# Seven 16-head attention stages: VectorE's small work per tile in another order, with the aggregation one slot later

## The reference, cut to what matters

```
q, k, v = x @ Wq (+bq), src @ Wk (+bk), src @ Wv        # src is x or the context
p = softmax(q @ k.T / sqrt(8))                          # 16 heads, 64 keys, some with a mask
o = (p @ v)                                             # denominators come out of the same matmul
x = layernorm(x + o @ Wo (+bo))                         # mean and variance over 128 features
```

## Time and profile before

| what | value |
|---|---|
| median of 3 runs | 4357.68 us (4356.09 to 4358.32) |
| span of the profiled execution | 4443.1 us, granted PE clock 0.914 over all of it |
| busy over the span | PE 3746.7, PEld 2747.7, DVE 3214.4, ACT 2236.5, POOL 1618.2 us |
| L0a, 21 to 340 us | PE busy 300.9 of 319 us, DVE 284.3, ACT 184.3, POOL 186.8 |
| L0x, 374 to 708 us | PE busy 302.2 of 334 us, DVE 274.8 |
| L1x, 1806 to 2106 us | PE busy 291.0 of 300 us, DVE 248.3 |
| L1f, 2123 to 2383 us | PE busy 256.5 of 260 us, DVE 228.2 |
| L2a, 2723 to 3038 us | PE busy 300.5 of 315 us, DVE 274.1 |
| L2x, 3057 to 3320 us | PE busy 256.6 of 263 us, DVE 229.3 |
| L3x, 3943 to 4303 us | PE busy 334.8 of 360 us, DVE 321.6, POOL 191.7 |

### The profile page before, as it was taken

One profiled execution on the slowest core, in us unless ns is written; L12 is line 12 of the kernel. 1 busy time (PEld: TensorE's weight loads), 2 busy tenths in 40 slices (PEclk: granted clock), 3 DMA queues, 4 the chain that ended last, 5 costly groups with the idle time before them and its releaser, 6 DMA issues. The chain is left out here.

```text
span 4443.1 us, 137315 instructions
## 1 busy us (share of the span) xinstructions
PE 3746.7 (84%) x48696; PEld 2747.7 (62%) x48696; DVE 3214.4 (72%) x7860; ACT 2236.5 (50%) x4080; POOL 1618.2 (36%) x2677
## 2 busy tenths in 40 slices
PE   8997997588369999899998775998999778879986
PEld 6775666355257877677676553776774344457764
DVE  7996886224468888688786267887886677769975
ACT  4554553234334444566784344656873355535553
POOL 4663343633611111122354442332222244435544
PEclk9998997799789999999997887999999888889998
DMA  2011112466410000111001760000102100000001
GB/s 75 26 34 47 38 36 60 131 195 173 117 32 1 0 0 0 37 42 37 17 17 35 215 177 16 14 14 24 33 26 66 37 0 0 0 18 23 22 16 38
DMA packets 293801, 209.56 MB, mean 47 GB/s; under 512 B 51136, under 2 KB 272192, under 8 KB 293440
## 3 DMA queue, kind: packets, MB, share of 16 engines
q1 hardware_dynamic: 233760, 157.72, 12.4%
q0 software_dynamic: 12288, 25.19, 1.9%
q10 hardware_dynamic: 47520, 23.60, 1.8%
HBM read 122.49 MB, written 54.53 MB: 40 GB/s over the span
## 5 line engine op out<-in xcount | busy, mean ns | idle before, releaser
L1354 DVE TENSOR_TENSOR L0f_G<-L0f_SG,L0f_psH 128x512 f32<-128x512 f32 x106 | 73.0, 689 | 230.2 <-ACT L0f_SG L1098 138.4
L2223 POOL TENSOR_TENSOR L1a_rs<-L1a_ag,eps 128x1 f32<-128x1 f32 x64 | 12.1, 190 | 475.8 <-DVE L1a_ag L2383 475.8
L937 POOL DMA_INDIRECT L0f_sorted_x<-X,L0f_IDX x128 | 123.3, 963 | 86.7 <-issue 34.1
L958 POOL DMA_INDIRECT L0f_YG<-L0f_sorted_y,L0f_IDY x128 | 124.5, 973 | 80.4 <-DMA L0f_sorted_y<-L0f_YB 43.2
L2310 PE MATMUL L1a_psO<-L1a_WO,L1a_OT 128*64 128x128 f32 x2048 | 125.9, 276 | 6.3 <-ACT L1a_OT L2334 5.0
L2244 PE MATMUL L1a_psF<-L1a_XT,L1a_WQ 128*128 128x256 f32 x512 | 130.6, 389 | 0.5 <-DVE L1a_KT L2199 0.5
L1032 PEld LDWEIGHTS L0f_psO<-L0f_WB,L0f_G 128*128 128x128 f32 x848 | 107.4, 197 | 37.0 <-issue 37.0
L2310 PEld LDWEIGHTS L1a_psO<-L1a_WO,L1a_OT 128*64 128x64 f32 x2048 | 110.6, 137 | 24.3 <-ACT L1a_OT L2334 22.8
L1914 PE MATMUL L3a_psH<-L3a_UT,L3a_WG 128*128 128x512 f32 x128 | 81.4, 722 | 50.1 <-DVE L3a_G L2027 48.6
L586 ACT ACTIVATE L3x_PT<-L3x_psP 128x512 f32<-128x512 f32 x128 | 69.5, 595 | 100.9 <-PE L3x_psP L521 100.9
L1032 PE MATMUL L0f_psO<-L0f_WB,L0f_G 128*128 128x128 f32 x848 | 108.6, 280 | 8.0 <-issue 8.0
(11 more groups left out here) (684 smaller groups left out, 12981.2 us busy)
## 6 DMA issues: line engine op xcount, KB each, us to landing
L0f_WB<-in_w12a SPq DMA_DIRECT2D x53, 312.0 KB
L0f_XB<-L0f_sorted_x SPq DMA_DIRECT2D x53, 256.0 KB
L0f_sorted_y<-L0f_YB ACTq DMA_DIRECT2D x53, 256.0 KB
L1m_WB<-in_w12b SPq DMA_DIRECT2D x37, 321.0 KB
L1m_XB<-L1m_sorted_x SPq DMA_DIRECT2D x37, 256.0 KB
L1m_sorted_y<-L1m_YB ACTq DMA_DIRECT2D x37, 256.0 KB
L0f_sorted_x<-L0f_AC SPq DMA_DIRECT2D x27, 256.0 KB
L1m_sorted_x<-L1m_AC SPq DMA_DIRECT2D x27, 256.0 KB
```

The lines of the kernel that those rows point to most:

```text
L937: nc.gpsimd.indirect_dma_start(out=sorted_x[p][:, :], out_offset=bass.IndirectOffsetOnAxis(ap=IDX[:, k, t:t + 1], axis=0), in_=X[:, t, :], ...
L958: nc.gpsimd.indirect_dma_start(out=YG[:, b % 4, k, t % TB, :], out_offset=None, in_=sorted_y[p][:, :], in_offset=bass.IndirectOffsetOnAxis ...
L1354: nc.vector.tensor_tensor(G[0:f, J % 2, c, :], SG[0:f, c, :], up, ALU.mult).then_inc(S["g_ready"].sem, 1)
```

## The change

In `small` the order becomes: reciprocal of T-2, aggregation of T-5 (whose statistics were taken in the slot before), normalised output of T-2, residual sum of T-4, [second norm's sum in L3x], statistics of T-4. The output of a pair and POOL's work for it move one slot later, since the aggregation does; that puts the output into slots of the other parity (from even to odd in L0a, L0x, L1x and L2a, from odd to even in L1f, L2x and L3x). The mean squares of L0a move two slots later, and L0a unrolls four more slots of tiles and loops 11 turns instead of 12. The drain of each stage is one slot longer, in L0a two.

```diff
-def long_pipeline(eng, slot, drain):
+def long_pipeline(eng, slot, drain, first=8):
-    first, turns = 8, 12
+    turns = (56 - first) // 4
...
-            drain = 5 + e + late + (1 if affine is not None else 0) + (2 if tally else 0)
+            drain = 6 + e + late + (1 if affine is not None else 0) + (3 if tally else 0)
...
-                        F = T - 5 - e - late
+                        F = T - 6 - e - late
...
-                        Z, Y = T + 4, T - 7
+                        Z, Y = T + 4, T - 9
...
                     def small(T):
-                        A, J = T - 2 - late, T - 4 - e - late
+                        A, J, H = T - 2 - late, T - 4 - e - late, T - 5 - e - late
...
                             nc.vector.reciprocal(rden[:, A.par], o3[:, :, 2 * HD:VW]).then_inc(S["recip"].sem, 1)
+                        if H.ok:
+                            made(dv, "bn", H.t + 1)
+                            pace(nc.vector, S)
+                            nc.vector.bn_aggr(mv[:, H.u, H.par, :], st6[:, H.par, :]).then_inc(S["stats"].sem, 1)
+                        if A.ok:
+                            made(dv, "recip", A.t + 1)
+                            made(dv, "o_ready" if ln_o else "o_turned", A.t - 1)
+                            nc.vector.tensor_tensor(ON[:, A.par, :].rearrange("p (b h d) -> p b h d", h=2, d=HD),
+                                                    o3[:, :, 0:2 * HD].rearrange("p b (h d) -> p b h d", h=2),
+                                                    rden[:, A.par].unsqueeze(3).to_broadcast([P, HP, 2, HD]), ALU.mult).then_inc(S["normed"].sem, 1)
...
                             nc.vector.tensor_tensor(RB[:, J.u, J.par, :], psJ, res, ALU.add).then_inc(S["res"].sem, 1)
-                        if A.ok:
-                            made(dv, "recip", A.t + 1)
...
-                        if J.ok:
-                            made(dv, "res", J.t + 1)
-                            nc.vector.bn_stats(st6[:, J.par, :], RB[:, J.u, J.par, :]).then_inc(S["bn"].sem, 1)
...
                         if J.ok:
-                            made(dv, "bn", J.t + 1)
-                            pace(nc.vector, S)
-                            nc.vector.bn_aggr(mv[:, J.u, J.par, :], st6[:, J.par, :]).then_inc(S["stats"].sem, 1)
+                            made(dv, "res", J.t + 1)
+                            made(dv, "stats", J.t - 1)
+                            nc.vector.bn_stats(st6[:, J.par, :], RB[:, J.u, J.par, :]).then_inc(S["bn"].sem, 1)
...
-                        A = T - 5 - e - late
+                        A = T - 6 - e - late
```

More of the change, by code:

```diff
@@ L322, in slot @@
                             sp.dma_start(CR[:, N.u, :], io["ctxT"][:, bass.ds(N.p * 256, 256)]).then_inc(parity_sem("ctx_in", N), 16)
-                    long_pipeline(sp, slot, drain)
+                    long_pipeline(sp, slot, drain, 12 if tally else 8)
                     if arrive:
@@ L425, in slot @@
                             mean_squares(Y.p, X[:, bass.ds(Y.p * 2, 2), :], 1, MS[:, Y.u, :], "stat2_root", "means2")
-                    long_pipeline(g, slot, drain)
+                    long_pipeline(g, slot, drain, 12 if tally else 8)
                 @block.tensor
@@ L555, in slot @@
                             nc.tensor.matmul(psJ, OT[:, A.par, :], o, start=True, stop=True).then_inc(S["proj"].sem, 1)
-                    long_pipeline(pe, slot, drain)
+                    long_pipeline(pe, slot, drain, 12 if tally else 8)
                 @block.scalar
@@ L607, in slot @@
                             rows_of_x(M)
-                    long_pipeline(act, slot, drain)
+                    long_pipeline(act, slot, drain, 12 if tally else 8)
                 @block.vector
@@ L710, in slot @@
                             m.then_inc(S["out_rows"].sem, 1)
-                        for V_, par, mean, st, tallied, rooted in ((T + 3, 1, MC, stat2, "means", "stat_root"), (T - 8, 0, MS, stat, "means2", "stat2_root")):
+                        for V_, par, mean, st, tallied, rooted in ((T + 3, 1, MC, stat2, "means", "stat_root"), (T - 10, 0, MS, stat, "means2", "stat2_root")):
                             if tally and T.par == par and V_.ok:
@@ L720, in slot @@
                             nc.vector.tensor_scalar(MF[:, M.u, :], MI[:, M.u, :], 0.0, None, ALU.not_equal).then_inc(S["mask_used"].sem, 1)
-                    long_pipeline(dv, slot, drain)
+                    long_pipeline(dv, slot, drain, 12 if tally else 8)
             S.advance(dict.fromkeys(("xs", "rstd", "var_eps", "out_rows", "f_tx", "f_k", "f_q", "f_v", "o_tx", "o_k", "o_q", "o_v"), PAIRS))
```

## The result

| | median, us | lowest to highest | runs |
|---|---|---|---|
| before | 4357.72 | 4356.09 to 4358.32 | 4 |
| after | 4308.65 | 4300.37 to 4309.4 | 4 |

The ratio is 0.9879, interval 0.9867 to 0.9891: 49 us faster, forecast 33. A second measurement of the same kernel beside experiments gave 4303.91 (4297.26 to 4311.76; before there 4356.83), ratio 0.9874 (0.9856 to 0.9892).

A forecast was written before the change was run, and what follows sets the result against it. PE and DVE pass a token in L2a, L0a and L3x (9.91 us per pair in L2a, PE alone 9.47). Terms 17 + 10 + 3 = 30 us, 34 with half the loop edge back; 33 taken, 4325 us, range 4305 to 4347.

The forecast's parts named there:

- The token loop: L2a, L0a, L3x: PE and DVE wait for each other once per pair; 9.91 us in L2a, 8.84 after.
- the odd loop of 9.56: L0a: loop from odd scores including the reciprocal of mean squares, 0.1 us over PE's own time, left to rounding.
- rivals 1 and 2: 1: PE's chain through ACT holds the pair, 4350 to 4358, chance 0.09. 2: output waits for POOL, about 4385, 0.04.
- Rival 3: Loop body: new dependent DVE neighbours cost 0.44 us instead of 0.32, smaller gain, 4335; chance 0.20.
- Rival 4: All waits vanish and the loop edge costs nothing in L0a and L2a: 43 us, 4314; chance 0.12.
- I take the whole 7.2, since L3x shows it in the same code.: L0a and L2a: loop edges cost up to 0.3 us per turn, subtracted from 24.3 us, leaving 17.
- In these four nothing that DVE does sooner can be passed on, or very little.: L0x, L1x, L1f, L2x: 1 to 5 us from the odd slot near a loop edge, 3 taken.
- two waits of PE: L3x: 0.45 us for rope before V's projection and 0.12 from projection to scores, about 10 us gained.
- the output alone takes 0.52 us out of that slot: L3x, behind the odd residual sum: output, aggregation and normalised output leave the slot, covering both of PE's waits.
- DVE's total: DVE's work per slot: 0.24 us removed, at most 0.24 added, gain 0 to 0.1, only slack.
- The drain rule: Skill's flush after every VectorE instruction: loop saving would be 0.43 us instead of 0.55, DVE's work would not shrink.
- 4410 for the span of the next profile: Profiled span of 4443.1 us, 2% above the runs' median, less the forecast 33 us.

The follow-up runs named there:

- order_only: Kernel before with the residual sum put behind the normalised output, aggregation still right behind the statistics, no shift by a slot; 4371.36 us, ratio 1.0032.
- extra_work3: Changed kernel with VectorE writing zeros to an unread 128x384 scratch behind each tile's statistics, 448 times; 4367.63 us, ratio 1.0028.
- turn8: Changed kernel with loops turning every eight slots instead of four, and a semaphore instruction ahead of POOL's large operations; 4303.51 us, ratio 0.9874.
- output_later: Kernel before with output, drain and tally one slot later as in the change, order inside a slot unchanged; 4340.75 us, ratio 0.9967.
- sum_first: Changed kernel with the residual sum back ahead of the normalised output, aggregation still between reciprocal and residual sum; 4320.0 us, ratio 0.9907.

## Why the prediction was right in direction and too small

**The token loop was read rightly.** Both engines waited for each other once per pair, the loop through the residual sum was 9.91 us, and PE's own 9.47 came next. Measured after: 9.46 in L2a, and 9.51 in L0a, where in the odd slots the scores still start 0.15 us after the end of the shift and 0.37 to 0.39 after the projection (medians of the loop): the odd loop of 9.56 that the forecast let pass as rounding. DVE's piece measured 0.55 for 0.52. Of the rivals 1 and 2 nothing shows: the list of waits has none of PE between 2640 and 2880 us in L2a and between 60 and 300 us in L0a, and an output waited for POOL once per stage (in L1f twice), by 0.5 to 2.7 us, and nowhere inside the stretches of L0a, L2a and L3x read here. Rival 3's cost exists (in the loops of L1x, L1f, L2a and L2x of order_only the reciprocal and the output that needs it are 0.37 us or more apart), but an aggregation stands there in the changed kernel, and extra_work3 shows that L2a would not have noticed. Rival 4, no edge cost in L0a and L2a, is what happened in those two stages; it had been given 0.12 and 4314 us, and the median came out lower still.

**The step that failed: "I take the whole 7.2, since L3x shows it in the same code."** L0a and L2a gave 26.7 us. The gross sum of the forecast was 24.3, and the subtraction was wrong: turn8 shows no edge cost in these two stages. L3x and L0x have it for a reason of their own. There PE's last wait before the branch, for ACT's copy, is released late, and what the sequencer still has to do before the next scores comes after it; in L0x before, 1.07 us pass from that release (500.58) to the scores (501.65):

```profile
500.69 0.41 PE L434 MATMUL L0x_psF<-W,L0x_XS 128*128 128x128 f32 x2 [0.46 <-ACT L0x_CT L600]
500.93 0.39 PE L555 MATMUL L0x_psP<-W,L0x_OT 128*128 128x128 f32 x2
501.65 0.69 PE L482 MATMUL L0x_psS<-KB,L0x_QT 32*64 32x256 f32 x16 [0.33 <-issue]
```

In L0a and L2a of the changed kernel the lists named above have no such wait. That turn8 shortened L0x by 3.2 us bears it out; that this is the reason was only read from the trace. The stages gave 48.6 us for the forecast's sum of 30 (33 was that with half of the edge given back). Of the 18.6 missed this term is 7.2, and 2.4 more are in the periods: the shifts of L2a and L0a now lie 9.41 and 9.45 us apart per pair over the whole stage, under the 9.47 that was taken as PE's floor from one pair.

**The second, and the larger: "In these four nothing that DVE does sooner can be passed on, or very little."** Forecast 3 us, measured 12.2 (8.0 by the second pair of profiles), of it 4.7 in L2x, 4.1 in L0x, 2.2 in L1f. I had taken "PE busy 120.00 of 120" in L1f for a bound and L2x for a case of the same; L2x was busy 118.41 of 120 (3120 to 3240 us), and is 120.00 now. What the four stages had can be read from start-to-start times. In the loops of L2x before, the scores came 0.32 to 0.34 us after the projection in three slots of four, and 0.55 to 0.73 us in the first slot of each turn; in the changed kernel it is 0.32 in all. Before, and now:

```profile
3187.95 0.39 PE L555 MATMUL L2x_psP<-W,L2x_OT 128*128 128x128 f32 x2
3188.52 0.69 PE L482 MATMUL L2x_psS<-KB,L2x_QT 32*64 32x256 f32 x16 [0.18 <-issue]
```

```profile
3068.47 0.39 PE L555 MATMUL L2x_psP<-W,L2x_OT 128*128 128x128 f32 x2
3068.78 0.69 PE L482 MATMUL L2x_psS<-KB,L2x_QT 32*64 32x256 f32 x16
```

Over the loops that is 3.4 of the 4.7 us: a cost at the loop's edge, but in a stage for which the forecast had none, and one that DVE's earlier work removed. output_later alone removed it too (0.32 us in that slot, L2x -2.9). Which of PE's waits was released late there isn't shown. In L0x, PE's wait for ACT's copy of x's rows ahead of L445, 2.4 us in 12 waits, is down to 0.5 in one; of the stage's 4.1 us 1.2 lie in the loops, 1.3 in the first slots and 1.6 in the last. L1f's 2.2 and L1x's 1.2 us are near what a stage varies by, though four slots of L1f went from 16.18 to 16.09 us with PE busy 120.00 of 120 in both.

**L3x was right in size (9.6 for 10), in part by luck.** The forecast had two waits of PE, 0.45 us for rope (8.1 us in 18 pairs) and 0.12 at the scores (2.2). Start to start over the 24 pairs of the loops, product to V's projection fell from 30.4 to 22.8 us, a gain of 7.6; the odd scores come 0.22 us after the projection instead of 0.45 (medians), a gain of 5.3; and product to L441 rose from 25.0 to 29.5, a loss of 4.5 that the forecast didn't have. So one term was right, one too small and one missing, and the last two in part cancel. The cause is also narrower than written: "the output alone takes 0.52 us out of that slot" was the largest part of it, but output_later has the output gone and wins 1.4 us in L3x, and sum_first has the aggregation gone from behind the statistics as well and stands at 354.6, 2.2 above before. The output lands in the slot of L441, and PE waits for rope there. The gain is there only when the normalised output is also ahead of the wait.

**DVE's total.** The price of the neighbours was right (0.31 to 0.33 and 0.44 us in order_only). What I had not seen is that DVE is close behind PE in L1f and L2x, by 0.24 us per slot as extra_work3 has it; an order that had added more than it removed would have lost there, as order_only did.

**The drain rule.** The trace kept against it: 0.20, 0.31 and 0.43 us behind the same statistics, by what follows. The Trainium skill, "VectorE: DVE Perf Modes", section "The DRAIN you can't avoid", has every VectorE instruction followed by a flush of the pipeline, tied by a semaphore or not; the same section adds that a next instruction that isn't held starts earlier, which the prediction left out. By the flush alone order_only would have cost nothing and the change's new order would have saved less. The runs don't agree with that: order_only lost 14 us.

**The span.** "4410 for the span of the next profile": it was 4298.6. The step was that the 85 us by which the profiled span lay above the median would come again. They were that execution's own: every later span lies 2 us or less below its run's time, and most of the excess was in the work between L0x and L1x.

**How the gain adds up.** By the sums of the seven stages: output_later -15.4 us; from there to sum_first, which moves the aggregation away from the statistics, another -21.0; from there to the changed kernel -12.1, of which 11.9 in L3x. That is the 48.6.

## What to carry to other kernels

- Where two engines wait for each other by turns, add up the loop through both and compare it with each engine's own period; what counts is the work between the wait of one and the signal to the other, and an edit that looks like reordering can take it out of there. Small work that needs nothing goes ahead of a cross-engine wait.
- On DVE, put an independent small instruction between a producer and its consumer, and count neighbours before a group is reordered: the residual sum behind the normalised output took the kernel 14 us up in order_only, and 11 us down in the changed kernel against sum_first, where the aggregation stood elsewhere.
- A cost seen in one stage (here a loop's branch) is not in another because the code is the same: look for what releases the last wait before it. And don't read a busy share of 100% as no waits; compare start-to-start times.

## What the runs showed of the hardware that I had not expected

- A semaphore instruction between two dependent DVE instructions costs 0.12 us (0.31 to 0.43), though it computes nothing that they need.
- 0.41 us of extra DVE work per slot, 26 us to a stage, cost L2a 0.1 us in all and L3x 28.9 us.
- Two edits that each gave nothing in L3x (342.7 and 342.6 us) gave 7.7 us together (335.0; 335.0 again in the second measurement): each alone moved PE's marked waits from one place to another (14.7 us in the changed kernel, 15.8 and 15.1 with one edit), both halved them (7.6).
